# The second down projection as one Strassen product, and the squares of a norm partly summed on VectorE

## The reference

```python
# conditioned block: F = 1376, low-rank parts of rank 16 chosen per batch item, scaled by 0.5
gate = x @ W_gate.T + lora;  up = x @ W_up.T + lora
y = (silu(gate) * up) @ W_down.T + lora
# second block: I = 1792, RMS norm in front
nx = y * rsqrt(mean(y * y) + 1e-5) * ln_w
z = (silu(nx @ gate_w.T) * (nx @ up_w.T)) @ down_w.T
return x + z
```

## Time and profile before

| | |
|---|---|
| median of 3 runs | 439.57 us (439.55 to 439.87) |
| the profiled execution, its own time | 439.17 us |
| its span | 437.5 us |
| TensorE busy | 425.4 us, 1878 matmuls |
| VectorE busy | 274.5 us |
| ScalarE busy | 211.8 us |
| DMA | 29.38 MB, mean 67 GB/s |

### The profile page before, as it was taken

The page is one execution under the profiler, slowest core; times in us unless marked ns, Lnnn a source line. Parts: engine busy times, 40 slices in busy tenths (PEclk is TensorE's granted clock), DMA queues, the critical chain, the costliest instruction groups (busy, mean ns, idle before and its releaser), DMA issues.

```text
span 437.5 us, 5245 instructions
## 1 busy us (share of the span) xinstructions
PE 425.4 (97%) x1878; PEld 345.6 (79%) x1878; DVE 274.5 (63%) x400; ACT 211.8 (48%) x323; POOL 2.0 (0%) x7
## 2 busy tenths in 40 slices
PE   8999999999999999999988999999999989999996
PEld 5788888888877887787766788888888868888885
DVE  3899868787846367647499776858686459223001
ACT  5698675756553367404356455564545563220000
POOL 1000000000000000000000000000000000000000
PEclk9999999999999999999999999999999999999999
DMA  7610254111103310200100232222231010002402
GB/s 282 189 60 0 75 138 122 48 54 52 58 30 105 93 70 0 96 1 0 49 1 0 82 136 73 73 72 72 94 124 50 0 63 11 0 1 84 131 1 97
DMA packets 14780, 29.38 MB, mean 67 GB/s; under 512 B 2466, under 2 KB 4898, under 8 KB 14754
## 3 DMA queue, kind: packets, MB, share of 16 engines
q1 hardware_dynamic: 14466, 28.65, 20.3%
q10 hardware_dynamic: 288, 0.39, 0.2%
HBM read 26.94 MB, written 2.10 MB: 66 GB/s over the span
## 4 chain that ended last, share of the span: by engine, by line
PE 94%; DVE 3%; DMA 1%; issue 1%; ACT 0%; DVEq 0%
PE bank L1017 43%; PE bank L1189 32%; PE bank L1119 8%; PE bank L1148 3%; PE bank L1027 2%; PE bank L1204 2%; PE bank L1155 1%; DMA xsum_c<-wsh_in 1%; PE bank L1217 1%; DVE xs L653 1%; PE bank L1210 1%; DVE nx L839 0%; PE bank L1209 0%; DVE mu L685 0%; ACT xs L325 0%
## 5 line engine op out<-in xcount | busy, mean ns | idle before, releaser
L1017 PE MATMUL bank<-xs,ws 128*128 128x512 f32 x840 | 197.2, 390 | 2.4 <-DVE ws L653 1.7
L1017 PEld LDWEIGHTS bank<-xs,ws 128*128 128x128 f32 x840 | 155.6, 188 | 34.1 <-DVE ws L653 2.1
L1189 PE MATMUL bank<-xs,wdf 128*128 128x512 f32 x336 | 76.6, 389 | 1.6 <-DVE xs L653 1.6
L1189 PEld LDWEIGHTS bank<-xs,wdf 128*128 128x128 f32 x336 | 63.0, 188 | 15.0 <-issue 1.9
L1189 PE MATMUL bank<-xs,wdc 128*128 128x512 f32 (+1 forms) x264 | 64.6, 393 | 1.3 <-DVE xs L653 1.3
L1189 PEld LDWEIGHTS bank<-xs,wdc 128*128 128x128 f32 (+1 forms) x264 | 48.9, 188 | 13.1 <-issue 3.1
L653 DVE TENSOR_TENSOR xs<-act,xs 128x512 fp32r<-128x512 f32 (+1 forms) x50 | 32.5, 687 | 24.6 <-ACT xs L325 24.6
L1119 PE MATMUL bank<-xs,ws 128*128 128x512 f32 x192 | 45.2, 391 | 1.7 <-DVE xs L653 1.7
L325 ACT ACTIVATE xs<-act 128x512 fp32r<-128x512 f32 (+1 forms) x50 | 29.2, 622 | 34.4 <-PE bank L1189 29.9
L1119 PEld LDWEIGHTS bank<-xs,ws 128*128 128x128 f32 x192 | 35.6, 188 | 9.6 <-DVE xs L653 2.2
L653 DVE TENSOR_TENSOR ws<-wraw,ws 128x768 fp32r<-128x768 f32 (+1 forms) x28 | 24.2, 880 | 25.4 <-ACT ws L325 25.3
(11 more groups left out here) (89 smaller groups left out, 355.7 us busy)
## 6 DMA issues: line engine op xcount, KB each, us to landing
wraw<-wgu_in SPq DMA_DIRECT2D x24, 512.0 KB, 3.3
wdr<-wd_in SPq DMA_DIRECT2D x25, 256.0 KB, 3.3
xres<-xT_in SPq DMA_DIRECT2D x8, 256.0 KB, 3.4
out<-xres SPq DMA_DIRECT2D x7, 256.0 KB, 2.0
xa<-xT_in SPq DMA_DIRECT2D x3, 512.0 KB, 7.0
bgu_raw<-bgu_in SPq DMA_DIRECT2D x32, 32.0 KB, 2.0
ad_raw<-ad_in SPq DMA_DIRECT2D x8, 88.0 KB, 2.2
xa<-xT_in SPq DMA_DIRECT2D x2, 256.0 KB, 4.7
```

The source lines that it names most:

```text
L1017: ins = mm(z[:, :], ws[:, j % 2, w, s, k * P:(k + 1) * P], xs[:, c, r, k, :], start=(start and k == 0 and s == 0 and r == 0), stop=(k == 1 ...
L1189: ins = mm(z[:, :], wd[0:rows, s, h * P:(h + 1) * P], x[r][0:rows, :], start=(start and s == 0 and r == 0), stop=(stop and s == 1), skip_g ...
```

## The change

The second down projection becomes one Strassen-Winograd product over halves: outputs 0 to 255 and 256 to 511, depth tiles 0 to 6 and 7 to 13, tokens 0 to 511 and 512 to 1023. There are seven products of KF = 7 items, and an item is six matmuls (two output tiles, three passes). Three products take plain weight blocks, `vj_in`, in three loads of 896 KB, split during the down projection (`hi_j`, `lo_j`, 128x256 per item). Four take the plain block or sums kept in `vs`: in seven of the groups (`VS_AT`) VectorE makes four adds in place in `wdr` (`sums_v`), ScalarE and VectorE split 128x1024 (`hi_v`, `lo_v`). The per-group load and split of `wdf` are gone. Four products take combined activations, made in place by VectorE (`down_sum`, 28 of 128x512, the first seven, `nt1`, in the odd groups up to 17, before group 8 and after group 19). ScalarE copies six banks between products; the residual is built up in stages. The splits of an item come in the order shown.

The squares: ScalarE now makes the squares 0 to 2 of a half, VectorE adds them (`add_square`), and the sum is split and takes two matmuls; the fourth square is treated as before. So a half takes four matmuls in place of eight.

```diff
+VS_AT = {8: 0, 9: 1, 11: 2, 12: 3, 14: 4, 15: 5, 17: 6}
 # sync
-            for n in range(2):
-                load_wd(FC + n)
+            def load_v(k):
+                if k >= 1:
+                    sp.wait_ge(s_vlo, k)
+                sp.dma_start(vraw, vs_in[k].rearrange("p (a m) -> p a m", a=4)).then_inc(s_v_ld, 16)
+            load_v(0)
             for g in range(S1, S2 - 2):
+                if g - 1 in VS_AT:
+                    load_v(VS_AT[g - 1] + 1)
                 load_w(w_of(g + 2))
-                load_wd(FC + g - S1 + 2)
+            for j in range(3):
+                if j == 0:
+                    sp.wait_ge(s_walo, G2)
+                    sp.wait_ge(s_wblo, G2)
+                else:
+                    sp.wait_ge(s_jlo, KF * j)
+                sp.dma_start(jraw[:, 0:KF, :], vj_in[j].rearrange("p (k m) -> p k m", k=KF)).then_inc(s_j_ld, 16)
...
+            for h in range(4):
+                sp.wait_ge(s_res, h + 1)
+                sp.dma_start(out[1, :, h, :], xres[:, h, :]).then_inc(s_out[h], 16)
+                sp.wait_ge(s_out[h], 16)
+                sp.dma_start(xres[:, h, :], xT_in[0, :, h, :]).then_inc(s_xr_ld[h], 16)
 # scalar
             for j in range(S1, S2):
                 group(j, S2)
-                hi_wd(FC + 2 + j - S1)
+                if j in VS_AT:
+                    hi_v(VS_AT[j])
+            def hi_v(k):
+                a.wait_ge(s_vsum, 4 * k + 4)
+                copy(vs[:, k, :, 0, :], vraw).then_inc(s_vhi, 1)
 # vector
+            def sums_v(k):
+                v.wait_ge(s_v_ld, 16 * (k + 1))
+                for q, (to, more) in enumerate(((3, 0), (0, 1), (1, 3), (2, 1))):
+                    if q >= 1:
+                        v.wait_ge(s_vsum, 4 * k + q)
+                    nc.vector.tensor_tensor(vraw[:, to, :], vraw[:, to, :], vraw[:, more, :], ALU.add).then_inc(s_vsum, 1)
+            def lo_v(k):
+                v.wait_ge(s_vhi, k + 1)
+                v.wait_ge(s_vsum, 4 * k + 4)
+                sub(vs[:, k, :, 1, :], vraw, vs[:, k, :, 0, :]).then_inc(s_vlo, 1)
@@ group
+                if j in VS_AT:
+                    sums_v(VS_AT[j])
                 if j % 2 == 1:
                     c11(j)
                 c12(j)
+                if j in VS_AT:
+                    lo_v(VS_AT[j])
...
             for j in range(S1, S2):
                 group(j, S1, S2)
-                lo_wd(FC + 2 + j - S1)
-            lo_af(0)
+                if j % 2 == 1 and j < S2 - 1:
+                    down_sum("nt1", 1 + (j - S1) // 2)
+            for i in range(2):
+                lo_j(i)
+                lo_down(i)
             c22_sum(S2 - 1)
             c22_act(S2 - 1)
-            lo_af(1)
             c21(S2 - 1)
+            down_sum("nt1", KF - 1)
+            for i in range(2, 7 * KF):
+                p, k = i // KF, i % KF
+                if i % KF == 0 and p == 4:
+                    for h in range(4):
+                        with_copy(h, *((s_dcu, du2, ALU.add) if h < 2 else (s_dcm, dm5, ALU.subtract)))
+                elif i % KF == 0 and p == 5:
+                    for h in range(2):
+                        residual(h, 3, DG_BANK, ALU.add, False)
+                elif i % KF == 0 and p == 6:
+                    for h in range(2, 4):
+                        residual(h, 4, DB_BANK, ALU.subtract, False)
+                if p in (2, 4, 6) and k == 0:
+                    down_sum(("nt2", "t3", "t4")[p // 2 - 1], 0)
+                if p in (0, 5, 6):
+                    lo_j(KF * (0, 5, 6).index(p) + k)
+                if p in (2, 4, 6) and k + 1 < KF:
+                    down_sum(("nt2", "t3", "t4")[p // 2 - 1], k + 1)
+                lo_down(i)
 # tensor
-                    ins = down(Z_BANK[t][h], wdf[:, n, :, :], (slot_f(u, 0), slot_f(u, 1)), h, P, n == 0, n == FF - 1)
+            def down_item(i, tiles=range(2)):
+                p, k = i // KF, i % KF
+                for h in tiles:
+                    for s, r in PASSES:
+                        ins = mm(DOWN[p][3][h][:, :], down_w(i, s)[:, h * P:(h + 1) * P], slot_f(i, r),
+                                 start=(p < 2 and k == 0 and s == 0 and r == 0), stop=(k == KF - 1 and s == 1),
+                                 skip_group_check=True)
+            for i in range(7 * KF):
...
+                pe.wait_ge(s_alo, 22 + i + 1)
+                if i < 7 * KF - 3:
+                    ins = down_item(i)
+                    ins.then_inc(s_use, 1)
+                if i == 1:
                     p4(S2 - 1)
+            for h in range(2):
+                for i in range(7 * KF - 3, 7 * KF):
+                    ins = down_item(i, range(h, h + 1))
+                ins.then_inc(s_z, 1)
```

More of the change, by code:

```diff
@@ L288, in _ @@
[L288 to L299, removed]
@@ new lines, in _ @@
+            for h in range(4):
[3 more added lines that the diff above has]
+                sp.dma_start(xres[:, h, :], xT_in[0, :, h, :]).then_inc(s_xr_ld[h], 16)
+            for h in range(3):
+                sp.wait_ge(s_res, h + 5)
+                sp.dma_start(out[0, :, h, :], xres[:, h, :]).then_inc(s_out[h], 16)
+            for q in range(2):
+                sp.wait_ge(s_res, 8 + q)
+                cols = slice(q * 256, q * 256 + 256)
+                sp.dma_start(out[0, :, 3, cols], xres[:, 3, cols]).then_inc(s_out[3], 16)
@@ L309, in _ @@
+            for h in range(3):
+                sp.wait_ge(s_out[h], 32)
             sp.wait_ge(s_out[3], 48)
@@ L607, in _ @@
                 keep_y(m)
+            for m in range(3):
+                square(m)
+            hi_ac(20)
+            sum_hi(0)
             square_hi(0)
[L609 to L612, removed]
             hi_ac(21)
@@ L620, in _ @@
             hi_x(1, X21, nx0[:, 2:4, :])
-            for m in range(4, 8):
+            for m in range(4, 7):
                 keep_y(m)
-                square_hi(m)
+                square(m)
+            sum_hi(1)
+            keep_y(7)
+            square_hi(1)
             rsqrt(1)
@@ L642, in _ @@
             hi_x(1, XT4, xsum_f[:, 3])
-            hi_wd(FC + 1)
             for j in range(S1, S2):
                 group(j, S2)
-                hi_wd(FC + 2 + j - S1)
-            for u in range(2 * FF):
-                hi_af(u)
+                if j in VS_AT:
+                    hi_v(VS_AT[j])
+            for i in range(7 * KF):
+                p = i // KF
+                if p in (0, 5, 6):
+                    hi_j(KF * (0, 5, 6).index(p) + i % KF)
+                if i % KF == 0 and p >= 2:
+                    if p == 2:
+                        copy_q1()
+                    elif p == 3:
+                        copy_g()
+                    elif p == 4:
+                        copy_u2()
+                hi_down(i)
         @block.vector
@@ L980, in _ @@
                     unit_mul(2 + i)
-            lo_wd(FC)
             unit_mul(6)
@@ L999, in residual, with with_copy @@
-            def residual(m, cols):
-                v.wait_ge(s_xr_ld[m % 4], 16 * (m // 4 + 1))
-                v.wait_ge(s_z, m + 1)
-                part = xres[:, m % 4, cols]
-                nc.vector.tensor_tensor(part, part, Z_BANK[m // 4][m % 4][:, cols], ALU.add).then_inc(s_res, 1)
-            for m in range(7):
-                residual(m, slice(0, CH))
+            down_sum("nt1", KF - 1)
+            def with_copy(h, ready, kept, op):
+                v.wait_ge(s_xr_ld[h], 16)
+                v.wait_ge(ready, h % 2 + 1)
+                nc.vector.tensor_tensor(xres[:, h, :], xres[:, h, :], kept[:, h % 2, :], op).then_inc(s_pre, 1)
@@ new lines, in residual @@
+            def residual(h, product, bank_of, op, second, cols=slice(0, CH)):
+                if product < 6:
+                    v.wait_ge(s_use, product_end(product))
+                else:
+                    v.wait_ge(s_z, h - 1)
+                if second:
+                    v.wait_ge(s_xr_ld[h], 32)
+                else:
+                    v.wait_ge(s_pre, h + 1)
+                part = xres[:, h, cols]
+                nc.vector.tensor_tensor(part, part, bank_of[h % 2][:, cols], op).then_inc(s_res, 1)
@@ L1007, in _ @@
             for h in range(2):
-                residual(7, slice(h * 256, h * 256 + 256))
+                residual(h, 5, DA_BANK, ALU.add, True)
+            residual(2, 6, DB_BANK, ALU.subtract, True)
+            for q in range(2):
+                residual(3, 6, DB_BANK, ALU.subtract, True, slice(q * 256, q * 256 + 256))
         @block.tensor
```

287 lines of the change are left out of this document (180 added, 107 removed).

## The result

The changed kernel took 454.13 us (median of 4 runs, 453.01 to 454.86), the kernel before 439.62 beside it (439.55 to 439.87): a ratio of 1.0327, 95% interval 1.0302 to 1.0352. It is 14.5 us slower, where 5.2 were forecast, and lies outside the range of 440.5 to 449.5. The profiled execution is the slowest of the four, with a span of 452.8 us against 437.5, so 15.3 more. Executions that were disturbed as a whole count in no median or ratio here: two of the thirteen of `e2_squares_only`, 537.91 us at a granted clock of 0.751 (the profiled one) and 1261.83 us.

What follows compares the result with a forecast made beforehand. TensorE, busy 425.4 of 437.5 us, was taken as the bound. Groups +12.0, down projection -6.1 and squares -0.7 summed to +5.2 us, giving 444.8 us; range 440.5 to 449.5.

Steps and rivals of the forecast that it cites:

- the restarts: TensorE resuming after a stop: 0.05 us behind the semaphore in the sum, 0.26 as bound, making the groups' stalls 13.5.
- The bound and the direction: Whole kernel: TensorE's pace and VectorE's slack before its waits decide; slower by 5.2 us, chance of slower 0.82.
- The groups: Feed-forward groups: new weight work delays c22_sum, stalling TensorE in groups 9, 10, 12, 13, 15, 16, 18; 12.0 us together.
- The two additions for a late ScalarE: Groups 10 and 16: ScalarE's silus push lo_b later, making stalls of 2.14 and 2.22 us instead of 2.07.
- The clock: Whole kernel: granted clock expected to stay 1.0; falls entered only as a rival.
- Rival 3: Six gaps over 2 us each lower the clock, costing 2.3 us each, 14 in all: 459 us; chance 0.04.
- The down projection: Second down projection: 42 fewer matmuls (-9.52 us), earlier start -0.25, stops +2.5 and +1.35; taken as -6.1.
- the load of 896 KB: Third plain-weight load, before the last product: lands in 5.25 us, TensorE stands 1.35 us before the last items.
- The tail: Last matmul to end: unchanged; stores and reloads of xres queue behind the 896 KB load, ending near 423.
- The squares: Squares of the norm: 16 matmuls become 8, with a wait of 1.1 to 1.3 us; -0.7 us in all.
- Rival 1: The groups hide the new weights: with no stall 432.8 us; chance 0.13, plus 0.05 for a tie.
- Rival 2: Lateness compounds: late ScalarE costs each group with new weights another 0.7 us, groups 10 and 16 don't recover; 450 us, chance 0.12.

Runs made afterwards that it cites:

- e2_squares_only: The kernel before with only the change's squares edit: 439.28 us, ratio 0.9991.
- e3: The kernel before, with VectorE repeating a weight split four times at the end of five odd groups: 457.18 us, ratio 1.0392.
- e4: The kernel before, with VectorE repeating a weight split three times at the end of five odd groups: 448.34 us, ratio 1.0201.
- e1: The changed kernel with the new weights' adds and splits moved into VectorE's idle slots, the seventh block into the down projection: 434.96 us, ratio 0.9892.
- e5: e1 with the squares' lines of the change undone: 434.36 us, ratio 0.9864.
- e6: e5 with item 2 split before c21(19), the last nt1 sum after item 5, products 5 and 6's plain weights split earlier: 430.57 us, ratio 0.9790.
- e9: e6 with item 3 too split before c21(19), and item 13's down_sum put before item 9's split: 429.83 us, ratio 0.9767.
- e8: e6 with the change's squares put back: 430.99 us, ratio 0.9799.

## Why the prediction was wrong, point by point

**The sum of it.** In the profiles the change cost 15.3 us, where the forecast had 5.2. Of the 10.1 between them, falls of the clock are 6.6 (four of 1.6 to 1.7), stops and restarts in the groups 2.0, the tail 0.7, the squares 0.3, the rest of the down projection 0.2 and the stretch before the squares, the same in both kernels, 0.2. Three of the four executions had a clock that fits three falls; without them the median of 454.1 would be about 449.3, just inside the range. So the step that failed is the clock, which the sum has at nothing; the restarts come second.

**The bound and the direction: right.** TensorE's pace and the slack before `c22_sum` decided, and the down projection's 42 matmuls did not pay for the stops.

**The groups: right in place and size, short by the restarts.** 12.0 us were forecast, 11.93 measured. The two additions for a late ScalarE (2.14 in group 10, 2.22 in group 16) didn't show: both stops were 2.07. The walk of an even group can be followed in the profile of the changed kernel; group 14 starts at 308.82 (`ca` at 310.20 less 1.38), and these are VectorE's rows with ScalarE's `hi_v` between them:

```profile
315.86 1.23 DVE L742 TENSOR_TENSOR ws<-wsum,ws 128x1024 fp32r<-128x1024 f32 x1 [1.04 <-ACT ws L359]
317.00 1.80 DVE L858 TENSOR_TENSOR wdr<-wdr 128x256 f32<-128x256 f32 x4
318.72 0.68 DVE L774 TENSOR_TENSOR act<-mu,bank 128x512 f32<-128x512 f32 x1
318.83 1.06 ACT L359 ACTIVATE vs<-wdr 128x1024 fp32r<-128x1024 f32 x1 [2.52 <-DVE wdr L858]
...
319.93 1.23 DVE L742 TENSOR_TENSOR vs<-wdr,vs 128x1024 fp32r<-128x1024 f32 x1 [0.53 <-ACT vs L359]
321.07 0.68 DVE L785 TENSOR_TENSOR act<-mu,bank 128x512 f32<-128x512 f32 x1
```

`lo_b` at 7.04, the adds at 8.18, `hi_v` from 10.01, `lo_v` at 11.11, the sum at 12.25; forecast were 7.04, 8.19, 9.98, 11.07 and 12.22. The term lacked what a restart costs beyond its idle time. I had 0.05 in the sum and 0.26 as a bound; it is 0.30 [e3, e4], so seven restarts are 2.1 us.

**The clock: the step that failed.** Rival 3 had "The granted clock was 1.00, the 2.4 GHz level, through this trace's idle gap of 1.7 us", and I took that as evidence that gaps of 2.1 us are harmless too, with a chance of 0.04 left. It was one mechanism, and I gave it all or nothing: six falls and 14 us, or none. The changed kernel had four falls, 6.6 us, three of them behind stops of 2.07 to 2.08 us, and e3 shows that stops of this length are enough for those. The evidence I used was thin: three stops (1.74, 1.72 and 1.55 us) of one execution, all shorter than what I forecast. The Trainium skill (TensorE: Matmul & The Clock Gate, "The HAM clock gate"), which the prediction cites, says that idle time lowers the clock and that sustained work brings it back. The trace agrees: 0.50 behind four stops, and 1.0 again while TensorE worked on. The same section of the Trainium skill also says that the moment of the change varies from run to run, since what sets it runs free of the kernel's start. The runs here agree: falls behind some stops of one length and not behind others, three or four of them per execution (clocks of 0.989 and 0.985, a fall being 0.004). So falls should have been priced as a share of the stops, and not as a case by themselves: in the two profiles that have stops of 2.07 to 2.13 us, the changed kernel and e3, 5 of 10 had a fall behind them.

**The down projection: right, within 0.2 us.** Up to its last matmul it gave back 5.9 us (5.4, and 0.4 before item 0), where 6.1 were forecast. Stops of 2.32 and 1.20 us against 2.5 and 1.35 forecast (the terms of the first add up to 2.57); the load of 896 KB, issued at 428.16, took 5.0 us to its first reader against 5.25. e1 and e5 have both stops too (2.32, and 1.27 and 1.20), and e6 and e9 show that reordering removes them.

**The tail: a step missed.** I wrote that the stores and reloads of `xres` queue behind the load of 896 KB and "end near 423". The timeline of the changed kernel, with SP's issues (SPq) and their readers, shows that they end at 449:

```profile
428.16 0.33 SPq L323 DMA_DIRECT2D wraw<-vj_in  x1
428.53 0.43 SPq L331 DMA_DIRECT2D out<-xres  x1
...
433.16 0.42 ACT L359 ACTIVATE ws<-wraw 128x256 fp32r<-128x256 f32 x1 [7.11 <-DMA wraw<-vj_in]
...
433.88 0.33 SPq L333 DMA_DIRECT2D xres<-xT_in  x1
...
445.77 0.33 SPq L333 DMA_DIRECT2D xres<-xT_in  x1
...
449.38 0.75 DVE L1157 TENSOR_TENSOR xres<-xres,bank 128x256 f32<-128x256 f32 x2 [2.20 <-DMA xres<-xT_in]
```

Each of four stores had to land before its reload was issued. The first took 5.35 us (428.53 to 433.88), beside the load of 896 KB, the others 3.5 to 3.8, each with a reload just ahead of it; I had counted 2.0 for a store. With the last reload's 3.6 the four pairs took 21 us. The last residual waited until 449.38, with its matmuls done at 448.49: some 0.7 us more behind the last matmul than before. In e6, where the stores came earlier, it waited for TensorE instead.

**The squares: too good by 0.3 us.** -0.7 forecast, -0.38 measured. One row that all kernels share shortly ahead of the squares, 24 matmuls, is this in the kernel before and in the changed one:

```profile
177.73 5.74 PE L1189 MATMUL bank<-xs,wdc 128*128 128x512 f32 x24
```

```profile
177.94 5.74 PE L1362 MATMUL bank<-xs,wdc 128*128 128x512 f32 x24
```

From its start to the end of the stop at 227 us it is 49.80 before and 49.42 after. The same stretch is 49.79 to 49.81 in all six profiles with the old squares, and 49.42 or 49.43 in all four with the new ones. What the medians show (-0.4 in e2, +0.6 in e1 against e5, +0.4 in e8 against e6) is blurred by falls and by the start: that row begins anywhere from 177.72 to 178.76 us. The stop before the sum of three squares was foreseen (1.1 to 1.3, measured 1.20), its restart was not: the 0.3 that are missing fit it.

**The rivals.** Rival 1 (the groups hide it) fell by the stops themselves; its argument by totals was true, and e1 shows the room that it speaks of. Rival 2 (lateness compounds) didn't occur: the groups 11, 14 and 17 are whole. Rival 3 occurred in part.

**What stays open.** What decides behind which stop of some 2 us the clock falls is open. So is why it fell behind 227.36 us in the changed kernel's profile, where the kernel before has the same stop of 1.7 us and never a clock under 0.999, and where it fell in three executions of e2 and two of e1. The squares' extra stop 14 us earlier is in both, but e8, which has it too, had no clock under 0.999 in five executions. About 0.14 us of each restart is unexplained, and so are the longer executions at full clock.

## What to carry to other kernels

Before work is added to a helper engine, find for each of the main engine's waits how much slack the helper has at that point of its queue. Here 0.79 us of slack decided, though VectorE was busy for only 71% of the span, and the same work placed in its idle slots cost nothing: 454 us became 435, and with the last stops gone 430, 2.3% under the kernel before. And price a stop of TensorE above its idle time: 0.3 us for each restart, and for stops of about 2 us another 1.6 in half of the cases, for the clock (5 of 10 in the groups, 2 of 4 before item 2, in the profiles here).

## What the runs showed of the hardware that I had not expected

- Five stops of 2.12 us, 21 to 23 us apart, with nothing else changed, were followed by a granted clock of 0.50 in two cases of the profiled execution (1.62 us lost each); five stops of 1.39 us in none.
- Executions of one kernel, with the same work and the same stops, differ by whole falls: in e1 433.9 and 434.1 us at a granted clock of 1.0, 435.8 and 436.0 at 0.996.
- A store of 256 KB landed in 2.0 us in the kernel before, in 3.5 to 3.8 us where a reload of 256 KB was issued 0.4 us ahead of it, and in 5.35 us right behind a load of 896 KB.
